# A graph transformer on one core: experts' rows gathered two units ahead in the second front, key maxima one step late, and the slice weights turned in the third aggregation instead of the last stage

## The reference, cut to what matters

```python
x = x + L0_gnn(xn, src, dst, ...) + L0_mix(xn)
x = x + L0_ffn(layernorm(x))                 # one expert of 32 for each node (argmax), two small products
xn = layernorm(x)
x = x + L1_gnn(xn, ...) + L1_mix(xn)         # two convolutions: xW[src] * weights, summed by dst
x = x + L1_ffn(layernorm(x))

# L1_ffn: slice attention
slice_weights = softmax((x_mid @ W_slice + b_slice) / temp, axis=-1)        # N x (8 heads * 64 slices)
slice_token = einsum('bhnc,bhng->bhgc', fx_mid, slice_weights) / (slice_weights.sum(axis=2) + 1e-5)
out_slice = attention over the 64 slice tokens of each head                 # small
out_x = einsum('bhgc,bhng->bhnc', out_slice, slice_weights)
return out_x @ W_out + b_out                                                # N x 256
```

## Time and profile before

| | us |
|---|---|
| median of 3 runs (4332.55 to 4352.53) | 4349.64 |
| the profiled execution: its own time | 4339.2 |
| its span, first to last instruction | 4337.3 |
| second front (1840 to 2030 of the span) | 190 |
| third aggregation (3086 to 4163) | 1077 |
| small attention over slices (4165 to 4210) | 45 |
| last stage (4210 to the end) | 127 |
| busy over the span: PE / DVE / ACT / POOL | 3033.6 / 1837.6 / 778.6 / 2623.3 |

### The profile page before, as it was taken

One profiled execution on the slowest core, in us unless ns is written; L12 is line 12 of the kernel. 1 busy time (PEld: TensorE's weight loads), 2 busy tenths in 40 slices (PEclk: granted clock), 3 DMA queues, 4 the chain that ended last, 5 costly groups with the idle time before them and its releaser, 6 DMA issues. The chain is left out here.

```text
span 4337.3 us, 41624 instructions
## 1 busy us (share of the span) xinstructions
PE 3033.6 (70%) x12930; PEld 2240.1 (52%) x12930; DVE 1837.6 (42%) x3295; ACT 778.6 (18%) x1753; POOL 2623.3 (60%) x2704
## 2 busy tenths in 40 slices
PE   3877777777777619966776766666577777677769
PEld 2655555555544505554565654444355555555547
DVE  3644444444435521143333333333255555555534
ACT  1411111111113202222111111000022222222211
POOL 1377777777720141154777777777577777777701
PEclk9988888888887555598889887878789999999869
DMA  2344444444433225454444433333344444444414
GB/s 64 108 125 131 131 134 135 131 131 123 119 81 106 73 77 146 129 187 136 118 118 119 119 109 105 107 108 109 93 119 125 126 132 124 125 123 125 120 47 144
DMA packets 290103, 507.95 MB, mean 117 GB/s; under 512 B 67710, under 2 KB 189083, under 8 KB 289734
## 3 DMA queue, kind: packets, MB, share of 16 engines
q0 software_dynamic: 127728, 350.94, 27.9%
q1 hardware_dynamic: 155576, 148.80, 11.0%
q10 hardware_dynamic: 6560, 5.33, 0.4%
HBM read 412.70 MB, written 91.87 MB: 116 GB/s over the span
## 5 line engine op out<-in xcount | busy, mean ns | idle before, releaser
L1288 PE MATMUL bank<-g,m 128*128 128x256 f32 (+1 forms) x4704 | 1561.2, 461 | 923.5 <-DMA g<-d_t,src_i 612.9
L1217 POOL DMA_INDIRECT g<-d_t,src_i x1568 | 1573.9, 1004 | 516.5 <-issue 516.2
L1288 PEld LDWEIGHTS bank<-g,m 128*128 128x128 f32 x4704 | 931.2, 224 | 1246.9 <-issue 541.8
L1217 POOL DMA_INDIRECT g<-d_xn,src_i x784 | 787.3, 1004 | 256.1 <-issue 256.1
L1239 DVE TENSOR_TENSOR eq<-iota,rel_f 128x1024 bf16<-128x1024 f32 x294 | 357.9, 1217 | 390.5 <-PE bank L1288 336.5
L1252 DVE TENSOR_TENSOR accT<-bank,accT 128x256 f32 x294 | 122.7, 417 | 615.5 <-PE bank L1276 615.2
L1242 DVE TENSOR_TENSOR m<-eq,ew_f 128x1024 f32<-128x1024 bf16 x294 | 360.0, 1225 | 10.1
L1223 ACT ACTIVATE s<-bank 128x256 f32<-128x256 f32 (+1 forms) x294 | 112.1, 381 | 981.7 <-PE bank L1288 526.0
L214 POOL TENSOR_TENSOR rsd<-ved,mhalf 128x2 f32<-128x2 f32 (+1 forms) x25 | 19.4, 774 | 242.1 <-DVE ved L208 242.1
L2019 POOL DMA_DIRECT2D d_ys<-y x80 | 43.3, 542 | 193.1 <-ACT y L2003 193.1
L169 POOL DMA_DIRECT2D out<-y x25 | 18.1, 724 | 201.6 <-DVE y L2341 201.6
(11 more groups left out here) (369 smaller groups left out, 4404.7 us busy)
## 6 DMA issues: line engine op xcount, KB each, us to landing
g<-d_t,src_i POOLq DMA_INDIRECT x1568, 2.8
g<-d_xn,src_i POOLq DMA_INDIRECT x784, 2.8
side_xn<-d_xn SPq DMA_DIRECT2D x96, 128.0 KB, 2.5
d_x<-x SPq DMA_DIRECT2D x48, 256.0 KB, 2.1
d_sw<-side_lg SPq DMA_DIRECT2D x48, 256.0 KB, 3.5
sw<-d_sw SPq DMA_DIRECT2D x24, 512.0 KB, 3.6
d_xs<-side_zero SPq DMA_DIRECT2D x80, 128.0 KB, 3.4
xt<-d_xs SPq DMA_DIRECT2D x80, 128.0 KB, 2.5
```

The source lines that it names most:

```text
L1217: pool.indirect_dma_start(g[n % RING][:, u, 0:D], None, table, bass.IndirectOffsetOnAxis(ap=k.src_i[:, t:t + 1], axis=0)).then_inc(gathere ...
L1288: ins = pe.matmul(b[:, 0:GW], m[o][:, u, :], g[r][:, u, :], start=(u == 0), stop=(u == GT - 1 and not count))
```

## The change

In the second front the lists get longer lags: the experts' rows are gathered two steps ahead of the addition, not one; `turn`, `products` and `turn_t` follow one step later; VectorE normalises first in a step and reduces the key maxima of an older unit after that; the store of t moves from GpSimd's queue to SP's. In the third aggregation each tile's softmax weights are turned by four transposes into bank 6 and copied by ScalarE into a half of wkv1, and the turned tile is stored in place of the plain one. The last stage loads the turned weights and has no transposes and no PSUM copies; products rotate over banks 4 to 7, two tiles to a bank, and the bias is added in one operation for each unit.

```diff
 class Slices:
-    XN, LG, SENT = 4, 4, 6
+    XN, LG, SENT = 4, 4, 7
...
+        self.swT = [k.wkv1[:, j, :].rearrange("p (q n) -> p q n", n=P) for j in range(2)]
+        self.stored = [st.sem(f"side_stored{j}") for j in range(2)]
...
-        self.pe = {2: [(self.sums, 5)], 6: [(self.turn3, 3)], 9: [(self.turn2, 2)], 11: [(self.logits, 3)], 13: [(self.mix, 2)]}
-        self.act = {0: [(self.root, 3)], 5: [(self.exp, 4)], 6: [(self.relu, 2)], 7: [(self.copy_xnT3, 3)], 10: [(self.copy_xnT2, 2)]}
+        self.pe = {2: [(self.sums, 5)], 4: [(self.turn_sw, 5)], 6: [(self.turn3, 3)], 9: [(self.turn2, 2)], 11: [(self.logits, 3)], 13: [(self.mix, 2)]}
+        self.act = {0: [(self.root, 3)], 5: [(self.copy_swT, 5), (self.exp, 4)], 6: [(self.relu, 2)], 7: [(self.copy_xnT3, 3)], 10: [(self.copy_xnT2, 2)]}
...
     def send(self, i):
-        sp.wait_ge(self.sw_done, i + 1)
-        sp.dma_start(tile_rows(self.d.sw, i, w), self.lg[i % self.LG][0:w, :]).then_inc(self.stored[i % self.LG], 16)
+        sp.wait_ge(self.swT_done, i + 1)
+        sp.dma_start(self.d.swT[i * P:(i + 1) * P, :].rearrange("p (q n) -> p q n", n=P)[:, :, 0:w], self.swT[i % 2][:, :, 0:w]).then_inc(self.stored[i % 2], 16)
...
     def logits(self, i, w):
         wait(pe, self.lg_done, i)
+        wait(pe, self.swT_done, i - 1)
...
     def below_max(self, i, w):
-        wait(dve, self.stored[i % self.LG], 16 * (i // self.LG))
+        wait(dve, self.sw_turned, i - self.LG + 1)
...
+    def turn_sw(self, i, w):
+        pe, k, lg = self.e_pe, self.k, self.lg[i % self.LG]
+        wait(pe, self.sw_done, i + 1)
+        wait(pe, self.lg_done, min(i + 2, NTILE))
+        for q in range(HEADS * SLICES // P):
+            ins = pe.transpose(k.bank[6][:, q * P:q * P + w], lg[0:w, q * P:(q + 1) * P], k.ident[0:w, 0:w])
+        ins.then_inc(self.sw_turned, 1)
+
+    def copy_swT(self, i, w):
+        act = self.e_act
+        wait(act, self.sw_turned, i + 1)
+        wait(act, self.stored[i % 2], 16 * (i // 2))
+        act.activation(self.swT[i % 2][:, :, 0:w], self.k.bank[6][:].rearrange("p (q n) -> p q n", n=P)[:, :, 0:w], ACT.Copy).then_inc(self.swT_done, 1)
...
 stage_second_front:
-        t = Slots(st, "t", [P, 2, D], dma="pool")
+        t = Slots(st, "t", [P, 2, D], dma="sp")
...
-                pipeline(sp, (load, 0), (store_x2, 2), (store_xn, 3))
+                def store_t(u):
+                    wait(sp, t_done, u.n + 1, gsp)
+                    t.store(sp, u, d.t1)
+                pipeline(sp, (load, 0), (store_x2, 3), (store_xn, 4), (store_t, 5))
...
-                pipeline(pool, (gather, 0), (lambda u: nm.root(pool, u, gpool), 1), (store, 3))
+                pipeline(pool, (gather, 0), (lambda u: nm.root(pool, u, gpool), 2))
...
-                pipeline(dve, (greatest, 3), (normalise, 2), (add_experts, 1))
+                pipeline(dve, (normalise, 3), (greatest, 5), (add_experts, 2))
...
-                pipeline(act, (own, 4), (scale, 3), (copy_xnT, 2))
+                pipeline(act, (copy_xnT, 3), (own, 5), (scale, 4))
...
-                pipeline(pe, (turn_t, 4), (products, 3), (turn, 2))
+                pipeline(pe, (turn, 3), (turn_t, 5), (products, 4))
...
 stage_out:
-        sw = Slots(st, "sw", [P, 2, HS], dma="sp")
-        swT = Slots(st, "swT", [P, 2, NC4, P])
+        swT = Slots(st, "swT", [P, 2, HS], dma="sp")
...
-                    free(sp, turned, u, gate=gsp)
-                    sw.load(sp, u, d.sw)
+                    free(sp, y_psum, u)
...
+                        sp.dma_start(swT[u][:], d.swT[at:at + BODY, :].rearrange("(j p) n -> p j n", p=P)).then_inc(swT.sem[u.j], 16)
...
-                pipeline(dve, (copy, 0), (add, 1))
+                pipeline(dve, (add, 0))
...
+                def product(u):
+                    swT.landed(pe, u)
+                    wait(pe, a_done, u.n - 3)
                     for j, w in enumerate(u.tiles):
                         for c in range(NC4):
-                            ins = pe.matmul(k.bank[2 + j][0:w, 0:D], swT[u][:, j, c, 0:w], k.mout[:, c, :], start=(c == 0), stop=(c == NC4 - 1))
+                            ins = pe.matmul(k.bank[4 + u.n % 4][0:w, j * D:(j + 1) * D], swT[u][:, j, c * P:c * P + w], k.mout[:, c, :], start=(c == 0), stop=(c == NC4 - 1))
                     ins.then_inc(y_psum, 1)
-                pipeline(pe, (turn, 0), (product, 1))
+                pipeline(pe, (product, 0))
```

More of the change, by code:

```diff
@@ L2334, in add @@
                     y.sent(dve, u)
-                    for j, w in enumerate(u.tiles):
-                        ins = dve.tensor_tensor(y[u][0:w, j, :], k.bank[2 + j][0:w, 0:D], k.bout[0:w, :], ALU.add)
-                    ins.then_inc(a_done, 1)
+                    b = k.bank[4 + u.n % 4]
+                    dve.tensor_tensor(y.part(u), b[0:u.w, 0:u.k * D].rearrange("p (j d) -> p j d", d=D),
+                                      k.bout[0:u.w, :].rearrange("p (a d) -> p a d", a=1).to_broadcast([u.w, u.k, D]), ALU.add).then_inc(a_done, 1)
                     wait(dve, a_done, u.n + 1)
```

50 lines of the change are left out of this document (13 added, 37 removed).

## The result

The changed kernel takes 4269.48 us (median of 4 runs, 4268.09 to 4270.9) against 4347.6 for the kernel before, run beside it (4 runs, 4332.55 to 4352.53): a ratio of 0.9826, 95% interval 0.9807 to 0.9845. The forecast was 4272. The profiled execution has an own time of 4268.09 and a span of 4266.3, so its span is 71.0 shorter than the 4337.3 of before. The forecast sum of the three terms was −71 too; the stages show that this is partly luck.

The account below looks back on a forecast made before the run. Limits: a loop through four engines in the second front, GpSimd's gathers in the third aggregation, TensorE in the last stage. Terms −45 + 6 − 32 = −71 from 4339.2 gave 4268.2; adjusted for run scatter, 4272 us, range 4254 to 4300.

Parts of the forecast that it names:

- Term A: Second front: reordered lists and the moved t store give 4.70 us a step, −45 us in all (bounds −48 to −36).
- it costs nothing only while TensorE is slower by 0.3: Second front: VectorE's uncovered 0.85 us wait for the root is free while its 4.34 loop stays under TensorE's 4.64.
- The last t store: End of the second front: the 106-row store, now on SP's queue, takes 2.6 us at some 41 GB/s; 2 us added.
- The start: Second front's start: two more gathers cost at most +1.3, unit 1's turn no longer waits for keys (some −5): −3.7.
- Term B: Third aggregation: added transposes and copy lengthen only rounds without gathers and the end, +6 us (bounds +3 to +12).
- The bound of +12: Third aggregation: upper bound of its +6 us cost, if the low clock stretches each piece.
- 27 us of transposes disappear in TensorE's 261.5 us of waiting: Third aggregation, while gathers run: added transposes priced at nothing, 27 us if the cover of gather waits were gone.
- Term C: Last stage: 24.5 units at 3.41 us, plus 2 for slow first ones, −32 us (bounds −34 and −16).
- DMA did not limit the second front: Rival, second front: DMA stops at 240 GB/s, a step takes 5.5 us, A = −27, time 4290; chance 0.15.
- Loads did not bound the last stage: Rival, last stage: stretched loads make a unit take 4.1 us, C = −16, time 4288; chance 0.08.
- the case of the other side: Third aggregation leaves the gathers' pace; 1.6 us above it eats the gains; slower 0.07, of which 0.02 beyond that point.
- The key maximum's bank: Rival, second front: bank 2 keeps a 6.6 us loop, A about +5, time 4322; no-gain chance 0.04.

## Why the prediction was right, and where it wasn't

**The whole.** 4269.48 against 4272: right. The span's −71.0 equals the forecast sum by luck: the second front gained 10 us more, and the second aggregation's gathers, unchanged code, took 11.2 more than in the one profiled run of before. Runs on the faster chips place those gathers anywhere from 1018.4 to 1036.5, and old and new front have the same ones side by side (1131.3 and 1131.9); the +11.2 is scatter, not an effect.

**Term A, −45 forecast, −55.0 measured.** The mechanism was right. That it is the order of normalisation and key maximum is shown by the kernel with the maximum first (167.8 us). Part of the gain is clock, which the term never named: its 6.78 us a step held the three slow periods of before, 4.7 us, and the first step after ran mostly at 0.50 and took some 1.9 more than the later ones. Three sizes were off:
- The step, "I take 4.70 for a step, near TensorE's row": 4.59 over the 23 steps. It gives −50.3 against −47.9. TensorE's own step is 4.33; the rows said so, since the weight loads of the earlier trace rows are 3.32 + 1.01 = 4.33, and the 4.64 between them held 0.31 of waiting. VectorE's loop, put at 4.34, is 4.39 to 4.62. So the roles were the other way round: "it costs nothing only while TensorE is slower by 0.3" named the right wait, and the condition did not hold. It costs 0.2 a step, which the steps of the kernel with the root a step early gain back, at the price of a later start.
- "The last t store [...] I add 2": wrong in its sign. Between the last turn and the next stage's gather lie 17.07 us where there were 17.70, and 21.30 in the kernel with the store on GpSimd's queue. So the deeper lists cost +3.6, charged with +4.3, and the store's move gives −4.2; −0.6 together against +6.3 forecast. The transfer itself was priced well (2.6 us, some 3 measured). I never asked what the old end cost: 8.27 us of idle VectorE, most of it after the rows had left, stood in the trace of before.
- The start: −4.1 against −3.7, as worked out.

**Term B, +6 forecast, +9.1 measured.** The mechanism was right for the rounds without gathers: with the copy later, the end is shorter than in any of the five kernels with it early. By rounds, from one group of sums to the next after the last gather:

| us | before | after | difference | forecast |
|---|---|---|---|---|
| first round | 10.56 | 11.88 | +1.3 | +1.4 |
| second | 10.26 | 12.63 | +2.4 | +1.4 |
| third | 7.49 | 9.53 | +2.0 | +1.4 |
| the rest to Tt, and the start | 22.25 | 25.67 | +3.4 | +2.1 |

Part of the excess goes with the clock. The same two rounds as stretches, of the kernel after and then of the one with the root a step early, which has the same code here:

```profile
4071.80:4083.68 11.88, 8.79 (x39) 6.15 (x38) 4.89 (x13) 5.60 (x10) 0.00 (x0) 0.86 0.06 23
4083.68:4096.31 12.63, 9.57 (x38) 6.34 (x37) 6.74 (x16) 5.26 (x9) 0.00 (x0) 0.73 0.06 21
```

```profile
4061.99:4072.18 10.19, 7.10 (x40) 5.39 (x38) 5.05 (x13) 5.59 (x10) 0.00 (x0) 1.00 0.07 27
4072.18:4082.09 9.91, 6.86 (x38) 5.06 (x37) 5.96 (x15) 5.25 (x9) 0.00 (x0) 1.00 0.07 27
```

With a granted clock of 1.00 these rounds take 10.2 and 9.9 us, with 0.86 and 0.73 they take 11.9 and 12.6; before they had 0.84 and 0.83. At nearly equal clock, then, the first round grew by 1.3, as forecast, and I put the second round's other 1.1 down to its lower clock. Where the clock falls in these rounds differs between runs of the same code: the end takes 56.80 to 60.39 us in the five kernels with this tail. The bound of +12 "if the low clock stretches each piece" was the right thing to allow for. The kernel with transposes done twice fits: its first four rounds ran at 1.00 and its end took 56.5. "27 us of transposes disappear in TensorE's 261.5 us of waiting" held on the faster chips, where the gathers took no longer and TensorE's waiting for them fell by 17. It is not shown for the first chip, where that waiting was only 28.6 us without the transposes.

**Term C, −32 forecast, −31.0 measured.** 24.5 units at 3.45 are 84.5 against 83.6, and with the slower first ones the products take 87.3 against 85.6. Loads land in 3.6 us as before.

**The rivals.** DMA did not limit the second front, and has room for one more block in each step. Loads did not bound the last stage. On the faster chips GpSimd never waited for TensorE in the third aggregation, so the case of the other side did not arise; on the first chip its gathers waited with and without the turned weights, as shown above. The key maximum's bank closed no loop. Of the signs named ahead, the steps (4.6 to 4.8) came out at 4.52 to 4.59, just below their range; weight loads were busy 84%, not near 90; the root's wait was 0.94, not 0.85; the last stage took 97.6, not 95.

**The rules on DMA.** The Trainium skill (DMA: Bandwidth & Descriptors, section "Specifications") gives 358 GB/s as a core's limit at the HBM. The 340 GB/s over 90 us, with no step slowed, lie below it, but single slices of 2.25 us in that run moved up to 390. The measurement decides: with this one core at work 358 was no bound over such times. Its rule on the spread of a DMA over 2 engines for 106 rows (section "Why a DMA increments its semaphore by 16 and not by 1") agreed with the 41 GB/s of the earlier trace rows, with the 25 to 49 GB/s of the t store on SP, and with the turned tile of 128 rows, which left at 224 to 321 GB/s. But what the end of the block cost was decided by the queue that the store left on.

## What to carry to other kernels

Where a step's loop runs through several engines, look in each engine's list for an instruction that waits late and stands ahead of one that another engine needs early: swapping those two was worth 32.5 of the 55 us here, and giving a small dependent operation a whole step of its own brought the steps down to TensorE's own work. Price the end of a block by the idle time that the trace already shows there and by the queue that the last store is on, not by the transfer's rate. And when one stage scatters by more than an edit is worth, compare the stages that the edit touches, from the same events, not the whole time.

## What the runs showed of the hardware that I had not expected

With a store of 106 rows on GpSimd's queue as its last transfer the block ended 8.1 us after the last copy, with it on SP's queue 3.5, although the rows had left 7.0 us before that end on GpSimd's queue and 0.8 on SP's. The DMA busy share reads 1.02 at 340 GB/s while nothing slows, so a share near 0.9 was no sign here that transfers limit. In the second front before, TensorE's clock fell to half in three of its periods (8.2 us in place of 6.6); after, with TensorE busy 98.8% of the steady stretch, the granted clock there is 0.99, and only the first step still holds the lower level. 784 gathers of one code and data took 1018.4 to 1036.5 us on the faster chips and 1129 to 1185 on the other, where single gaps from start to start reached 8.7 us against 2.3 and GpSimd waited over 100 us in the second and in the third aggregation for something else than its issue.
